# The second layer's two dot products as two rows of one product, turned over, and new places in the tables of two layers

## The reference, cut to what matters

```python
gfold = folded * gate                       # 8 x 512 tokens x 256
target = styleT @ style_w.T                 # one style row per batch element
cos = jnp.sum(l2norm(gfold) * l2norm(target), axis=-1, keepdims=True)
scale = cfg * (1.0 + cos) * 0.5
cfg_blend = gfold + scale * (target - gfold)
merged = jnp.concatenate([x, cfg_blend], axis=-1)
y = merged @ merge_w.T + merge_b
```

## Time and profile before

| what | value |
|---|---|
| median of 3 runs | 1957.49 us (1952.1 to 1957.84) |
| profiled execution | 1953.37 us, span 1951.6 us |
| busy share of the span | PE 88%, DVE 67%, ACT 57%, POOL 31% |
| mean granted clock of PE | 0.939 |

### The profile page before, as it was taken

How to read it: one execution, slowest core, us unless ns; L and a number is a source line. 1 busy time by engine, 2 the same in 40 slices (tenths; PEclk the granted TensorE clock), 3 DMA queues, 4 the chain that set the end, 5 groups by cost and what they waited for, 6 DMA issues and landing times.

```text
span 1951.6 us, 25700 instructions
## 1 busy us (share of the span) xinstructions
PE 1715.5 (88%) x8463; PEld 1015.6 (52%) x8463; DVE 1312.7 (67%) x2873; ACT 1112.6 (57%) x2118; POOL 611.0 (31%) x880
## 2 busy tenths in 40 slices
PE   2365576999989999988999999999999998999998
PEld 1144344667557657552445454544445444676766
DVE  5756877887876665577868686767686734656550
ACT  6644667878768763344675757565757564222221
POOL 0145655856645633610101010100001002334332
PEclk9755788989999999998999999999999999999999
DMA  9450000000000002303120303030303005000000
GB/s 375 123 167 1 24 6 20 20 1 20 15 1 14 20 4 67 66 18 68 26 47 11 61 2 71 2 68 5 68 5 68 5 3 152 3 11 22 12 22 22
DMA packets 94422, 83.57 MB, mean 43 GB/s; under 512 B 9881, under 2 KB 87842, under 8 KB 94034
## 3 DMA queue, kind: packets, MB, share of 16 engines
q1 hardware_dynamic: 94192, 81.91, 15.3%
q10 hardware_dynamic: 98, 0.03, 0.0%
HBM read 51.26 MB, written 5.09 MB: 29 GB/s over the span
## 4 chain that ended last, share of the span: by engine, by line
PE 41%; DVE 8%; ACT 6%; issue 1%; POOL 1%; POOLq 0%; DVEq 0%; ACTq 0%
PE k_psum L91 13%; PE k_psum L2536 6%; PE k_psum L2062 5%; PE k_psum L2123 5%; PE k_psum L2176 5%; PE k_psum L2053 4%; PE k_psum L97 3%; DVE l_small L2212 2%; ACT l_prob L2001 2%; ACT L2001 1%; ACT L2017 1%; ACT l_gu L2017 1%; DVE l_xn L2285 1%; DVE l_small L2199 1%; DVE l_xn L2287 1%
## 5 line engine op out<-in xcount | busy, mean ns | idle before, releaser
L2212 DVE TENSOR_REDUCE l_small<-k_psum 128x1 f32<-128x512 f32 x512 | 328.8, 684 | 124.6 <-PE k_psum L2176 121.7
L2001 ACT ACTIVATE l_prob<-k_psum 128x512 f32<-128x512 f32 x512 | 286.4, 596 | 196.6 <-PE k_psum L2053 193.4
L1985 POOL TENSOR_TENSOR k_x_res<-k_x_res,k_arena_a 128x256 f32<-128x256 f32 x32 | 23.3, 727 | 418.8 <-DVE k_arena_a L2256 418.8
L2062 PE MATMUL k_psum<-l_prob,l_v 128*32 128x512 f32 x1024 | 138.1, 612 | 0.2
L2123 PE MATMUL k_psum<-k_arena_a,l_gu 128*128 128x256 f32 x512 | 135.5, 393 | 0.7 <-ACT l_gu L2017 0.7
L91 PE MATMUL k_psum<-l_turned_over,k_arena_a 128*128 128x512 f32 x256 | 120.8, 596 | 4.2 <-ACT l_gu L2017 4.2
L91 PE MATMUL k_psum<-k_arena_b,l_w_f 128*128 128x512 f32 x256 | 123.9, 612 | 0.0
L1468 PE MATMUL k_psum<-l_w_f,k_arena_b 128*128 128x256 f32 x512 | 122.7, 386 | 0.2 <-ACT k_arena_b L1282 0.2
L91 PE MATMUL k_psum<-l_hT,k_arena_b 128*128 128x512 f32 x256 | 114.3, 592 | 0.0
L2536 PE MATMUL k_psum<-k_arena_b,l_gu 128*128 128x256 f32 x512 | 113.0, 379 | 0.0
L2123 PEld LDWEIGHTS k_psum<-k_arena_a,l_gu 128*128 128x128 f32 x512 | 97.9, 197 | 19.8 <-issue 2.2
(11 more groups left out here) (390 smaller groups left out, 3786.6 us busy)
## 6 DMA issues: line engine op xcount, KB each, us to landing
su_raw<-in_L_cond_wa SPq DMA_DIRECT2D x6, 1536.0 KB, 22.4
k_arena_b<-k_arena_c SPq DMA_DIRECT2D x32, 192.0 KB, 3.5
k_x_res<-in_x SPq DMA_DIRECT2D x1, 4096.0 KB, 19.7
k_arena_b<-k_arena_c SPq DMA_DIRECT2D x32, 128.0 KB, 3.2
out<-k_x_res SPq DMA_DIRECT2D x8, 512.0 KB, 2.9
l_mod_mlp<-mod SPq DMA_DIRECT2D x8, 384.0 KB, 3.6
l_qT<-k_arena_c SPq DMA_DIRECT2D x16, 192.0 KB, 3.7
l_kT<-k_arena_c SPq DMA_DIRECT2D x16, 192.0 KB, 3.2
```

The lines of the kernel that those rows point to most:

```text
L2001: act.activation(prob[:, s % 2, j, :], psum[:, 2 + n % 2, :], ACT.Exp, scale=float(HD) ** -0.5).then_inc(exp_ready.sem, 1)
L2062: last = pe.matmul(psum[j * BLOCK:(j + 1) * BLOCK, 4, :], v[e % 2][:, kt, at:at + BLOCK], prob[:, n % 2, j, :], start=(kt == 0), stop=(kt ...
L2212: dve.tensor_reduce(mx[:, n % T, n // T:n // T + 1], psum[:, s_bank(e, n), :], AX.X, ALU.max).then_inc(max_ready.sem, 1)
```

## The change

`dots` puts the style column and a column of zeros side by side as a stationary pair (and zeros and ones for the squares), and g and gsq are the moving side with 512 columns. Four products, eight instructions, leave two rows of 512 sums in bank 3. A new entry of ACT, `dots`, copies the two rows to SBUF (into the first row of z2); a new entry of PE, `dotsT`, turns them in four transposes so that each token's two sums lie beside each other; `gg` reads them from there. `style_pair` and `pair` take the place of `styleT` and `one`, and six semaphores of the setup become two.

```diff
     elif stage == "dots":
         pe.wait_ge(gsq_ready.sem, gsq_ready.at(e, KD))
-        for i in range(T):
-            mm(nc, psum[:, 3, i:i + 1], [(g[:, k, tok(i)], styleT[:, k, e:e + 1]) for k in range(KD)])
-        for i in range(T):
-            last = mm(nc, psum[:, 3, T + i:T + i + 1], [(gsq[:, k, tok(i)], one[:]) for k in range(KD)])
+        mm(nc, psum[0:2, 3, :], [(style_pair[:, k, e, :], g[:, k, :]) for k in range(KD)] + [(pair, gsq[:, k, 0:L]) for k in range(KD)]).then_inc(summed.sem, 1)
+    elif stage == "dotsT":
+        pe.wait_ge(sums_ready.sem, sums_ready.at(e, 1))
+        for i in range(T):
+            last = turn(nc, psum[:, 3, 2 * i:2 * i + 2], sums[:, tok(i)], ident[0:2, 0:2])
         last.then_inc(dots_ready.sem, 1)
...
+    elif stage == "dots":          # ACT
+        act.wait_ge(summed.sem, summed.at(e, 1))
+        ac.activation(sums, psum[0:2, 3, :], ACT.Copy).then_inc(sums_ready.sem, 1)
...
-        V.tensor_scalar(gg[:], psum[:, 3, T:2 * T], 1e-24, None, ALU.max).then_inc(gg_ready.sem, 1)
-        V.tensor_scalar(s[:], psum[:, 3, 0:T], cos_scale[:, e:e + 1], None, ALU.mult).then_inc(dots_taken.sem, 1)
+        V.tensor_scalar(gg[:], dots[:, :, 1], 1e-24, None, ALU.max).then_inc(gg_ready.sem, 1)
+        V.tensor_scalar(s[:], dots[:, :, 0], cos_scale[:, e:e + 1], None, ALU.mult).then_inc(dots_taken.sem, 1)
```

The tables change as follows (entries without their `ahead`, only the stretches that differ):

```diff
 PE, behind dots
-dots, gate 2, up 1, o 0, o 1, o 2, gate 3, up 2, merge 0, gate 4, up 3, o 3, setup, gate 5,
-mods 1, up 4, f1 0, up 5, gate 6, merge 1, gate 7, up 6, f1 1, up 7, merge 2, f1 2
+dots, gate 2, up 1, o 0, o 1, dotsT, o 2, gate 3, up 2, merge 0, gate 4, up 3, o 3, setup, gate 5,
+mods 1, f1 0, up 4, gate 6, merge 1, up 5, gate 7, f1 1, up 6, merge 2, up 7, f1 2
 PE, around turn
-f2 2, xq 2, f2 3, turn 0, proj 2, f2 4, turn 1, xq 3, f2 5, proj 3, pre 0
+f2 2, xq 2, f2 3, proj 2, f2 4, turn 0, xq 3, f2 5, turn 1, proj 3, pre 0
 ACT
-ssq 2, xT 0, proj 2, xl2 3, xT 1
+ssq 2, proj 2, xT 0, xl2 3, xT 1
-silu 1, silu 2, ssqo 0, ssqh 0, silu 3
+silu 1, dots, silu 2, ssqo 0, ssqh 0, silu 3
 DVE
-h 0, scan, x3 2, gg, stats 1, x3 3, h 1, xw 3, s, rinv, base 0, h 2, u 0, amax 3, u 1, h 3,
-merge 0, u 2, h 4, amaxh 0
+h 0, scan, x3 2, stats 1, x3 3, h 1, gg, xw 3, h 2, s, rinv, u 0, base 0, h 3, u 1, merge 0,
+h 4, u 2, amax 3, amaxh 0
```

More of the change, by code:

```diff
@@ L587 @@
     ("hT", 0, -2), ("ssq3", 1, -1), ("xq", 3, 1), ("ssq3", 2, -1), ("ssq", 1, 2), ("xl2", 0, 0), ("xl2", 1, 0), ("ssq3", 3, -1), ("hT", 1, -2),
[2 rows of a table removed]
[2 rows of a table added]
     ("z", 0, -1), ("fi", 0, 1), ("xq2", 0, 0), ("xq2", 1, 0), ("xq2", 2, 0), ("xq2", 3, 0), ("z", 1, -1), ("fi", 1, 1), ("xl", 1, 3), ("gsq", 0, -1),
-    ("fi", 2, 1), ("silu", 0, 0), ("fi", 3, 1), ("gsq", 1, -1), ("silu", 1, 0), ("silu", 2, 0), ("ssqo", 0, 1), ("ssqh", 0, 0),
+    ("fi", 2, 1), ("silu", 0, 0), ("fi", 3, 1), ("gsq", 1, -1), ("silu", 1, 0), ("dots", 0, -1), ("silu", 2, 0), ("ssqo", 0, 1), ("ssqh", 0, 0),
     ("silu", 3, 0), ("ssqo", 1, 1), ("ssqo", 2, 1), ("silu", 4, 0), ("ssqu", 0, 1), ("ssqo", 3, 1), ("ssqu", 1, 1), ("xl", 2, 3), ("ssq4", 0, -1),
@@ L598 @@
     ("fi", 0, 1), ("fi", 1, 1), ("pre", 1, -1), ("xq2", 0, 0), ("xq2", 1, 0), ("fi", 2, 1), ("gate", 0, 0), ("fi", 3, 1), ("up", 0, 0),
-    ("mods", 0, 1), ("f2", 6, -3), ("gate", 1, 0), ("f2", 7, -3), ("dots", 0, -1), ("gate", 2, 0), ("up", 1, 0), ("o", 0, 1), ("o", 1, 1),
+    ("mods", 0, 1), ("f2", 6, -3), ("gate", 1, 0), ("f2", 7, -3), ("dots", 0, -1), ("gate", 2, 0), ("up", 1, 0), ("o", 0, 1), ("o", 1, 1), ("dotsT", 0, -1),
     ("o", 2, 1), ("gate", 3, 0), ("up", 2, 0), ("merge", 0, -1), ("gate", 4, 0), ("up", 3, 0), ("o", 3, 1), ("setup", 0, 46), ("gate", 5, 0),
[2 rows of a table removed]
[2 rows of a table added]
     ("f1", 5, -2), ("xoq", 0, 1), ("xoq", 1, 1), ("y2", 0, 0), ("hq", 2, 0), ("yo", 0, 1), ("xoq", 2, 1), ("hq", 3, 0), ("f1", 6, -2), ("yo", 1, 1),
@@ L759, in layers01 @@
         b_merge, b_f2, gateT, style = sb("b_merge", [P, D]), sb("b_f2", [P, D]), sb("gateT", [P, KD, L]), sb("style", [P, D])
-        small = Small(sb("small", [P, 400]))
-        half, one = small(B), small(1)
+        small = Small(sb("small", [P, 416]))
+        half, pair = small(B), small(2)
+        one = pair[:, 1:2]
         bn, mv, var, rstd, away = small(T, 6), small(T, 2), small(T), small(T), small(T)
@@ L783, in layers01 @@
         z, z2, g = view(arena_b, Z_AT, KD, L + 3), view(arena_b, Z2_AT, KD, L + 2), view(arena_b, G_AT, KD, L)
-        gsq = z2
+        gsq, sums = z2, z2[0:2, 0, 0:L]
         junk_h = sb("junk_h", [P, FF])
@@ L976, in _ @@
                 gp.memset(half[:], -0.5).then_inc(half_ready, 1)
-                gp.memset(one[:], 1.0).then_inc(half_ready, 1)
+                gp.memset(one, 1.0).then_inc(half_ready, 1)
+                gp.memset(pair[:, 0:1], 0.0).then_inc(half_ready, 1)
+                gp.memset(style_pair[:, :, :, 1], 0.0).then_inc(half_ready, 1)
                 gp.memset(ones, 1.0).then_inc(half_ready, 1)
-                pool.wait_ge(half_ready, 3)
+                pool.wait_ge(half_ready, 5)
                 for stage, t, e in steps(POOL_TURN):
@@ L1378, in _ @@
                         last.then_inc(style_done, 1)
[L1379 to L1383, removed]
+                        pe.wait_ge(style_ready, SQUARES)
+                        mm(nc, psum[:, 3, 0:B], [(ones, style_sq[:, k, :]) for k in range(KD)]).then_inc(style_done, 1)
+                        pe.wait_ge(style_ready, COSINES)
+                        mm(nc, psum[0:B, 3, 0:D], [(styleT[:, k, :], w_merge[:, KD + k, :]) for k in range(KD)]).then_inc(style_done, 1)
                     elif stage == "mods":
@@ L1642, in _ @@
                         step.link(V.tensor_scalar(cfg[:], cfg[:], 0.5, None, ALU.mult))
[L1643 to L1649, removed]
+                        dve.wait_ge(style_done, SQUARES)
+                        step.link(V.tensor_copy(styleT, psum[:, 3, 0:KD * B].rearrange("p (k b) -> p k b", k=KD)))
+                        V.tensor_tensor(style_sq[:], styleT, styleT, ALU.mult).then_inc(style_ready, 1)
+                        dve.wait_ge(style_done, COSINES)
+                        V.tensor_scalar(cos_scale[:], psum[:, 3, 0:B], 1e-24, None, ALU.max).then_inc(style_ready, 1)
+                        dve.wait_ge(style_done, ROW)
+                        V.tensor_copy(row, psum[0:B, 3, 0:D]).then_inc(style_ready, 1)
                         dve.wait_ge(weights_loaded, 48)
@@ L1713, in _ @@
                     elif stage == "gg":
+                        dots = psum[:, 3, 0:2 * T].rearrange("p (t a) -> p t a", a=2)
                         dve.wait_ge(dots_ready.sem, dots_ready.at(e, 1))
```

21 lines of the change are left out of this document (11 added, 10 removed), and 14 rows, old and new, of tables (ACT_TURN, DVE_TURN, PE_TURN).

## The result

The changed kernel takes 1982.0 us (median of 4 runs, 1981.6 to 1982.4) against 1957.7 us of the kernel before beside it: ratio 1.0129, 95% interval 1.0108 to 1.0150. It is slower, by 24 us; 1958 had been forecast, with 1940 to 1974 as the range. The profiled execution has a span of 1980.6 us, 29.0 us more than that of before; some 5 of these 29 are there because the profiled execution of before (1953.37 us) was one of its shorter ones.

What follows compares the result with a forecast made beforehand. PE was taken to set the pace from the round of 556, before it a path through POOL, ACT, PE and DVE. Rounds +1.2 and new clock falls 3.4 make +4.6 on 1953.4: 1958.0 us, range 1940 to 1974.

Steps and rivals of the forecast that it cites:

- The product, the copy, the turn, the clock: At dots: product 3.43 us, ACT's copy 0.60, four turns 0.44, gg at 5.4, gate 2 and up 1 at full clock.
- Rival C: Behind dots: two loaded columns don't hold the clock, so the falls stay and 8.6 us are not won; 1967, chance 0.05.
- Its counter-argument: Against the clock falling behind dots: attention's products with 32 columns loaded run at 612 ns as full ones do.
- h 2 before s, u 0 late, o 3 idle: DVE's s held beside hw 0 until 9.7; up 3's 2.71 us wait goes; PE idles 2.0 us before o 3.
- Gate 6: PE idles 2.6 us before gate 6, for silu 5 behind h 4, u 2 and ssqu 2, up to round 628.
- the sum by rounds: Gains and costs added for the rounds from 262 to 757: together +1.2 us, with 3.4 us for new clock falls besides.
- Low clock as a credit: Half of the low-clock time comes back, such as 3.4 us in the round of 556 and 1.7 in that of 693.
- Merge 2: On PE merge 2 stands before up 7, of which 0.7 us was counted.
- Turn 0: Proj 2 and f2 4 fill PE's 2.86 us before turn 0; xq2 not earlier; can win half of 391.00's 3.41 fall.
- Behind the last dots: Round of 757: half of the 5.47 us at low clock comes back, less 0.5 for the clamp: -2.2 us.
- A: Faster: falls behind dots come back in full (13.7 us) and the wait before gate 6 costs nothing; 1940, chance 0.28.
- B: Slower: gate 6's 2.6 us wait brings the long clock fall each time, six of them 20.4 us; 1975, chance 0.27.

Runs made afterwards that it cites:

- Experiment 1: The changed kernel with silu 5 on ACT directly behind ssqo 3, ahead of ssqu 1, xl 2, ssq4 0 and ssqu 2: 1963.8 us.
- experiment 4: The kernel before with only the new product, its copy on ACT, its turn on PE, and gg behind h 1: 1962.7 us.
- experiment 7: The changed kernel's tables with the old product of 32 one-column instructions, no copy and no turn: 1993.1 us.
- experiment 6: The kernel before with new product, copy, turn, gg behind h 1, DVE's s, rinv, base 0 ahead of xw 3, POOL's hw 0 behind sgn 3: 1957.8 us.
- experiment 8: The changed kernel with PE's old order between mods 1 and f1 2, and turn 0, turn 1 and xT 0 in their old places: 1954.7 us.
- experiment 5: The kernel before with new product, copy, turn, gg behind h 1, and DVE's s, rinv and base 0 ahead of xw 3: 1965.6 us.

## Why the prediction was wrong, point by point

*The product, the copy, the turn, the clock: right.* 3.53 us to gate 2 against 3.43; the copy 0.59 against 0.60; four turns 0.34 from start to start of what follows against 0.44; gg 5.4 us after dots; no fall behind dots. Rival C is refuted: behind none of the eight dots does the clock fall. Its counter-argument was weaker than it looked: 1024 of the products with 32 columns take 138.1 us together at 612 ns each, so several of them run at once.

*h 2 before s, u 0 late, o 3 idle: right, a little too small.* s was held, o 3 waited 2.41 us where 2.0 stood. Not seen: the third instruction of s is held too (0.65 at 505.81; 0.17 in the round of 628 before), and with o 3 this puts h 4 at 14.8 instead of 13.8.

*Gate 6: the mechanism right, and the size nearly.* 2.38 us of idle PE in six rounds where 2.6 stood, ended by silu 5 behind ssqu 2, u 2 and h 4. The half clock behind it came in the three full rounds, 1.15 us of merge 1 and 0.4 of gate 6 each, where two falls in six rounds were counted. Experiment 1 takes wait and falls away together and gets 18 us.

*The step that failed is the sum by rounds.* The working had the root of h 26.8 us after dots, and used it in the rounds of 333, 408 and 481 only. From 556 on PE's own terms were added up, its old idle time as a credit, because "PE sets the pace from the round of 556 on", from a busy share of 60.81 of 63.60 us (693). A PE that is busy 95% of a round does not thereby set its length: in the round of 628 its busy time stayed (61.49, 61.44 us) and the round grew by 6.9. The path goes through PE's waits there too. The seven measured rounds are 24 us longer in all than the predicted ones (the 3.4 us that were counted for new falls stand outside these); 14 of the 24 lie in the rounds of 556, 628 and 693 (+3.1, +6.9 and +2.3 where -2.0, +1.8 and -1.7 stood), 10 in the four before.

In the round of 628 dots to root of h went from 21.43 to 27.54: h 3 comes 1.4 us later than before, by the held s, h 4 2.4 and h 5 5.4, behind gate 6's wait and merge 1. In that of 693 it went from 21.34 to 23.33; there u is gone, and merge 1 ahead of up 5 puts h 5 at 15.6 us after dots, where it was at 14.0, a term that the sum left out for that round. Part of it was in the trace: s takes 0.23 us in its second instruction in the round of 628 (634.17, experiment 4), so it ran free there; after the change its first instruction is held in that round (DVE of after):

```profile
656.59 2.31 DVE L1736 TENSOR_TENSOR l_small<-l_small 128x4 f32<-128x4 f32 x1
```
The earlier trace rows showed a held instruction in the rounds of 408 and 481, base 0 in the one and s in the other, and it was taken for the rule.

In the full rounds the path was the right one and mis-sized: h 5 comes 21.4 us after dots where 19.1 stood, by 1.0 us at h 4 and by 1.55 of half clock behind gate 6, and merge 2 adds the 0.7 counted. The round of 262, put at 0, grew by 2.5.

*Low clock as a credit: it came, and counted only in part.* Low clock between 262 and 860 us fell from 68.3 to 37.5 us. In the new tables, where PE's items lie on the path, that is worth 11 us (experiment 7); in the old tables, with hw 0 later, the new product gives 1957.8 us, the time of before (experiment 6), though the low clock is down there too, to 44.4 us: h 2, for which up 3 waits, still comes 9.6 to 9.9 us after dots, and up 3, which did not wait in the round of 408 before, stands 1.96 us for it in that of 407 here. What the clock gave at dots went into that wait.

*Merge 2: right* (0.7; 0.71 measured, and 0.98 at merge 3). *Turn 0: right*: the idle time before it went (2.86 to 0.47) without xq2 coming sooner, and what it won is the fall at 391 (18.52 to 16.96 in that round); not seen was its price in the round of 556, where root of h to turn 0 grew by 2.1 us, with PE busy up to turn 0 (back to 29.1 with the turns in their old places, experiment 8).

*Behind the last dots*: 0.9 us won where 2.2 had been counted.

The rivals: A needed gate 6's idle time off the path; experiment 1 shows it on it. B had the right sign and the right place, but not its price: six long falls were counted (20 us), and three short ones came, 1.55 us each. That its 1975 lies nearest to 1982 is luck; the wait itself, six times 2.38 us, is the larger part.

Of the 29 us, the 5.5 of the round of 408 are split by the experiments, root of h after dots: 29.1 as changed, 25.8 with silu 5 ahead, 25.1 with the merges back, 24.0 to 24.5 with f1 0 behind up 4 and silu 5 in its old place; 23.6 before (26.2 in the round of 481). So the cause of the loss is PE's new order between mods 1 and f1 2, together with u 2 behind h 4, on which silu 5 waits; u 2 put back alone was not run.

## What to carry to other kernels

Find the one stretch whose start and end every round has in common, cut all rounds there, and sum a change along it; a busy share near 100% does not say that an engine's own work sets the pace. Before an item is put in front of another on a queue, follow the wait behind it through all engines: here one entry moved on DVE (u 2 behind h 4) and two on PE (f1 0 ahead of up 4, up 5 behind merge 1) left a chain beside which PE had nothing to do. And look whether a small instruction will fall beside a long one of an engine that holds it; experiment 6 moved only POOL's long instruction out of the way, for 8 us.

## What the runs showed of the hardware

A DVE instruction on four elements per partition takes 0.23 us alone and 2.25 to 2.40 us if it starts beside POOL's 128x1024 product (2.34 us), and ends with it; h, which reads one operand from PSUM, ran beside it at its usual 0.75 (635.66 above). It goes both ways: POOL's root took 1.78 us beside a DVE product of two SBUF tiles and 1.01 without (experiments 4 and 5). This agrees with the Trainium skill, "SBUF — State Buffer", section "SBUF: two separate sides": one pair of ports is shared by the two engines as an exclusive lock for a whole instruction.

Products with two columns loaded and 512 moving were followed by no fall of the granted clock in any of the eight rounds, nor in the nine other kernels with that product (the first fall comes 11.3 us after dots or later), where 32 instructions of one moving column, about as long (3.49 to 3.91 us against 3.53), had lost it in six of eight and, in the new tables, in eight of eight (experiment 7). Idle stretches of PE of 2.4 us were followed by a fall to 0.50 in some rounds and not in others of the same kernel; which, was not settled.
